# Another order of all engines in the attention step, and two 128x512 products of constants ahead of its stack transposes

## The reference

```python
x = x + tanh(g_xattn) * xattn(layernorm(x), ctx, ctx, mask, ...)   # 16 heads of 8, rope on q and k
x = x + tanh(g_ffn) * ffn(layernorm(x), ...)                       # 8 experts, each token goes to one
# ffn: logits = x @ Wr + br; idx = argmax(logits); gate = softmax(logits)[idx]
#      out = gate * (gelu(x @ W1[idx] + b1[idx]) @ W2[idx] + b2[idx])
```

## Time and profile before

| | us |
|---|---|
| median of 3 runs (lowest, highest) | 294.68 (293.27, 297.7) |
| the profiled execution | 294.33 |
| its span, first to last instruction | 292.5 |
| busy: PE, DVE, ACT, POOL | 237.4, 188.7, 165.9, 178.2 |
| mean granted TensorE clock | 0.942 of full |

### The profile page before, as it was taken

How to read it: one execution, slowest core, us unless ns; L and a number is a source line. 1 busy time by engine, 2 the same in 40 slices (tenths; PEclk the granted TensorE clock), 3 DMA queues, 4 the chain that set the end, 5 groups by cost and what they waited for, 6 DMA issues and landing times.

```text
span 292.5 us, 13366 instructions
## 1 busy us (share of the span) xinstructions
PE 237.4 (81%) x5065; PEld 201.2 (69%) x5065; DVE 188.7 (64%) x638; ACT 165.9 (57%) x482; POOL 178.2 (61%) x221
## 2 busy tenths in 40 slices
PE   1257899888798898879888896788789899999960
PEld 1146777677676676757666675577679899999950
DVE  1636758788789669798888957775576444444420
ACT  1235758788667668567878675335364344444420
POOL 2275745756647859748898686711877755555550
PEclk9999979999799989799999999758999999999995
DMA  7899000303030401204000000132132533111100
GB/s 229 244 380 358 14 2 10 106 13 103 3 112 12 119 16 56 90 2 131 16 12 25 13 26 12 37 89 55 53 116 79 147 108 100 55 30 32 38 20 0
DMA packets 23729, 22.41 MB, mean 77 GB/s; under 512 B 3792, under 2 KB 19173, under 8 KB 23668
## 3 DMA queue, kind: packets, MB, share of 16 engines
q1 hardware_dynamic: 20388, 15.75, 17.6%
q0 software_dynamic: 2272, 4.46, 4.6%
q10 hardware_dynamic: 1008, 1.35, 1.4%
HBM read 16.50 MB, written 5.51 MB: 75 GB/s over the span
## 4 chain that ended last, share of the span: by engine, by line
PE 56%; DVE 19%; issue 11%; POOL 5%; ACT 3%; DMA 2%; SPq 0%; POOLq 0%; DVEq 0%; ACTq 0%
PE ps L734 12%; PE ps L788 10%; DVE mx L1227 8%; PE ps L778 5%; PE ps L745 5%; PE ps L764 5%; PE ps L763 3%; PE ps L717 3%; PE ps L715 3%; PE ps L716 3%; PE ps L810 2%; DMA x_all<-in_x 2%; PE ps L855 2%; PE ps L703 1%; POOL rows L501 1%
## 5 line engine op out<-in xcount | busy, mean ns | idle before, releaser
L549 POOL DMA_INDIRECT out<-fin,got x39 | 37.9, 972 | 27.5 <-DVE fin L1286 22.0
L1227 DVE TENSOR_REDUCE mx<-ps 128x16 f16<-128x1024 f32 x32 | 39.1, 1222 | 18.6 <-PE ps L745 18.1
L501 POOL DMA_INDIRECT rows<-x_all,dest_i x32 | 32.8, 1025 | 19.5 <-DVE x_all L1062 12.3
L734 PE MATMUL ps<-w_f,hT 128*128 x312 | 44.5, 286 | 0.0
L788 PE MATMUL ps<-vx,pr 128*64 128x32 f32 x1024 | 39.5, 234 | 2.8 <-DVE on L1162 2.4
L788 PEld LDWEIGHTS ps<-vx,pr 128*64 128x64 f32 x1024 | 36.0, 150 | 7.1 <-ACT pr L578 2.4
L734 PEld LDWEIGHTS ps<-w_f,hT 128*128 128x128 f32 x312 | 37.8, 191 | 1.0 <-issue 0.3
L528 POOL TENSOR_TENSOR rot<-qk,cf 128x256 f32<-128x256 f32 x32 | 23.4, 730 | 24.7 <-ACT qk L600 17.4
L515 POOL TENSOR_TENSOR stk<-rot,stk 128x256 f16<-128x256 f32 x32 | 21.7, 678 | 25.1 <-DVE stk L1240 25.0
L1286 DVE SCALAR_TENSOR_TENSOR fin<-ps,got 128x128 f32<-128x128 f32 x39 | 13.7, 350 | 36.0 <-PE ps L734 34.9
L578 ACT ACTIVATE pr<-ps 128x1024 f32<-128x1024 f32 x32 | 32.7, 1021 | 6.7 <-PE ps L832 6.7
(11 more groups left out here) (156 smaller groups left out, 615.4 us busy)
## 6 DMA issues: line engine op xcount, KB each, us to landing
got<-rows SPq DMA_DIRECT2D x39, 72.0 KB, 1.9
w_f<-in_W_rows SPq DMA_DIRECT2D x8, 256.0 KB, 3.1
w_r<-in_W_last_row SPq DMA_DIRECT2D x8, 256.0 KB, 4.3
w_f<-in_L_ffn_W SPq DMA_DIRECT2D x8, 256.0 KB, 4.7
x_all<-in_x SPq DMA_DIRECT2D x3, 512.0 KB, 8.3
xt_all<-in_x_t SPq DMA_DIRECT2D x3, 512.0 KB, 7.2
ct_all<-in_ctx SPq DMA_DIRECT2D x3, 512.0 KB, 7.5
out<-fin,got POOLq DMA_INDIRECT x39, 2.3
```

The lines of the kernel that those rows point to most:

```text
L501: pool.indirect_dma_start(out=rows, out_offset=bass.IndirectOffsetOnAxis(ap=dest_i[:, t:t + 1], axis=0), in_=x_all[:, t, :], in_offset=Non ...
L549: pool.indirect_dma_start(out=out_d, out_offset=bass.IndirectOffsetOnAxis(ap=got_i[:, u % GOT, R_ID:R_ID + 1], axis=0), in_=fin[:, u % FRI ...
L734: mm = pe.matmul(o, hT[:, par, c, :], w2_f[:, bass.ds(e, 1), c, :].rearrange("p o n -> p (o n)"), start=False, stop=(c == FC - 1))
L1227: dve.tensor_reduce(mx[:, t % 2, :].rearrange("p (w r) -> p w r", w=4)[:, :, 0:NA], ps_s[:, :].rearrange("p (w a k) -> p w a k", w=4, k=S) ...
```

## The change

Nothing that reaches the output is changed. What moves, in each attention step:

- PE: the transpose of the maxima of tile i-3 (it was tile i-2 at the step's end) and the onT transpose go right behind the projection; the PV product goes ahead of the stacks; the transposed scores go between the two halves of the scores. Ahead of the stacks, from tile 3 on, stand two products of a constant with a constant, 128x512 in fp16, into the bank that the stacks then overwrite (keep_warm).
- ACT: the copy of onT goes ahead of k, k ahead of lx, v ahead of kT and qT.
- DVE: x2 goes ahead of q; the casts hi go ahead of the maximum mx.
- POOL: the scatters go behind the rope.
- The transposed maxima move to bank 7, beside the PV product. For this PE waits for on before it writes the maxima, and for ACT's copy of them before PV. The values get a ring of their own, VRING = 5.

```diff
+VRING = 5
+WARM, WARM_FROM = 2, 3
-        vx = sb("vx", [P, RING, 2, 8, 32])
+        vx = sb("vx", [P, VRING, 2, 8, 32])
-        ps_mx = bank[5].bitcast(F16)[:, 0:P]
+        ps_mx = bank[7].bitcast(F16)[:, 4 * P:5 * P]
...
@@ POOL: step(i) @@
-                for _ in range(SCATTER_AT.get(i, 0)):
-                    scatter()
                 t = i
...
                     pool.tensor_tensor(rot[:, par, :], rot[:, par, :], rot_s[:, par, :], ALU.add).then_inc(rope_done, 1)
+                for _ in range(SCATTER_AT.get(i, 0)):
+                    scatter()
...
@@ ACT: step(i) @@
                     act.activation(mxT[:, t % 2, :], ps_mx, ACT.Copy).then_inc(mxT_ev, 1)
+                t = i - 5
+                if live(t):
+                    act.wait_ge(onT_done, t + 1)
+                    wait(act, op_done, t - 1)
+                    act.activation(onT[:, t % 2, :], ps_onT, ACT.Copy).then_inc(onT_ev, 1)
...
                     act.wait_ge(qe_ev, t + 1)
-                    act.activation(x_all[:, t, R_LOGIT:R_LOGIT + NE], ps_lx, ACT.Copy).then_inc(lx_ev, 1)
...
                     act.activation(qk[:, par, D:2 * D], ps_kv[:, 0:D], ACT.Identity, scale=mask_s[:, t:t + 1]).then_inc(k_ev, 1)
+                    act.activation(x_all[:, t, R_LOGIT:R_LOGIT + NE], ps_lx, ACT.Copy).then_inc(lx_ev, 1)
...
-                    wait(act, pv_done, t - RING + 1)
+                    wait(act, pv_done, t - VRING + 1)
...
@@ PE: step(i) @@
+            def keep_warm(n):
+
+                for _ in range(n):
+                    pe.matmul(bank[5], ident_h, ch[:, K_EXP:K_EXP + 512], start=True, stop=True)
...
+                t = i - 3
+                if live(t):
+                    pe.wait_ge(mx_done, t + 1)
+                    wait(pe, on_done, min(T, i - 4))
+                    wait(pe, mxT_ev, t)
+                    pe.transpose(ps_mx, mx[:, t % 2, :], ident_h).then_inc(mxT_done, 1)
...
+                t = i - 4
+                if live(t):
+                    s, par = t % VRING, t % 2
+                    pe.wait_ge(p_rdy, t + 1)
+                    pe.wait_ge(v_ev, t * 4 + 4)
+                    wait(pe, on_done, t)
+                    pe.wait_ge(mxT_ev, min(T, t + 2))
...
+                t = i - 1
+                if live(t):
+                    par = t % 2
+                    wait(pe, qT_ev, t)
+                    if t >= WARM_FROM:
+                        keep_warm(WARM)
...
-                t = i - 2
-                if live(t):
-                    pe.wait_ge(mx_done, t + 1)
-                    pe.wait_ge(qT_ev, min(T, t + 2))
-                    wait(pe, mxT_ev, t)
-                    pe.transpose(ps_mx, mx[:, t % 2, :], ident_h).then_inc(mxT_done, 1)
...
@@ DVE: step(i) @@
+                t = i - 6
+                if live(t):
+                    dve.wait_ge(op_done, t + 1)
+                    dve.wait_ge(lx_ev, t + 1)
+                    dve.tensor_tensor(x_all[:, t, 0:QX], ps_op, x_all[:, t, 0:QX], ALU.add).then_inc(x2_done, 1)
...
-                t = i - 2
-                if live(t):
-                    dve.wait_ge(s_done, t + 1)
-                    wait(dve, mxT_done, t - 1)
-                    dve.tensor_reduce(mx[:, t % 2, :].rearrange("p (w r) -> p w r", w=4)[:, :, 0:NA],
...
                     dve.tensor_copy(win[:, H:2 * H, :].rearrange("p h (c d) -> p h c d", c=4)[:, :, 1:4:2, :], k_f
                                     ).then_inc(hi_done, 1)
+                t = i - 2
+                if live(t):
+                    dve.wait_ge(s_done, t + 1)
+                    wait(dve, mxT_done, t - 1)
+                    dve.tensor_reduce(mx[:, t % 2, :].rearrange("p (w r) -> p w r", w=4)[:, :, 0:NA],
...
```

More of the change, by code:

```diff
@@ L608, in step @@
                     act.activation(tg[:, :], gates[:, :], ACT.Tanh).then_inc(s_tg, 1)
+                t = i
+                if live(t):
+                    s = t % VRING
+                    wait(act, pv_done, t - VRING + 1)
+                    if t == 0:
+                        act.wait_ge(s_v1, 2)
+                    v_ps = ps_kv[:, D:2 * D].rearrange("p (j hh d) -> p j hh d", hh=2, d=HD)
+                    for b in range(2):
+                        for hh in range(2):
+                            act.activation(vx[64 * hh:64 * hh + 64, s, b, :, 16 * hh:16 * hh + HD],
+                                           v_ps[64 * b:64 * b + 64, :, hh, :], ACT.Copy).then_inc(v_ev, 1)
                 t = i - 1
@@ L616, in step @@
                                    ).then_inc(qT_ev, 1)
-                t = i
-                if live(t):
-                    s = t % RING
-                    wait(act, pv_done, t - RING + 1)
[L621 to L628, removed]
-                if live(t):
-                    act.wait_ge(onT_done, t + 1)
-                    wait(act, op_done, t - 1)
-                    act.activation(onT[:, t % 2, :], ps_onT, ACT.Copy).then_inc(onT_ev, 1)
                 if i - 2 in EXPERT_AT:
@@ L765, in step @@
                     pe.matmul(ps_kv[:, 0:D], pick, bk_h[:, :], start=False, stop=True).then_inc(qkv_done, 1)
+                t = i - 3
[4 more added lines that the diff above has]
+                    pe.transpose(ps_mx, mx[:, t % 2, :], ident_h).then_inc(mxT_done, 1)
+                if i == 3:
+                    pe.wait_ge(s_vo, 64)
+                    pe.matmul(bank[4][:, 0:NE], wo_n[:, :], id_wr[:, P:QX], start=True, stop=True).then_inc(s_wox, 1)
+                t = i - 5
+                if live(t):
+                    if t == 0:
+                        pe.wait_ge(s_cs, 2)
+                    pe.wait_ge(on_done, t + 1)
+                    wait(pe, x2_done, t)
+                    if i - 3 in GROUP_AT:
+                        pe.wait_ge(g_read, GROUP_AT[i - 3] + 1)
+                    pe.transpose(ps_onT, on[:, t % 2, :], ident).then_inc(onT_done, 1)
+                t = i - 4
[5 more added lines that the diff above has]
+                    pe.wait_ge(mxT_ev, min(T, t + 2))
+                    for j in range(8):
+                        for b in range(2):
+                            mm = pe.matmul(ps_o[S * b:S * b + S, 32 * j:32 * j + 32], pr[:, par, NA * (j % 2) + j // 2, b, :],
+                                           vx[:, s, b, j, :],
+                                           start=True, stop=True)
+                    mm.then_inc(pv_done, 1)
                 t = i - 1
@@ L779, in step @@
                     mm.then_inc(stk_done, 1)
[L780 to L791, removed]
                 if tile(i - F0):
@@ L834, in step @@
                     mm.then_inc(st_done, 1)
+                t = i - 2
+                if live(t):
+                    pe.wait_ge(half_done, t + 1)
+                    scores(t, 1).then_inc(s_done, 1)
                 if i - 2 in GROUP_AT:
@@ L1164, in step @@
                                       ALU.mult).then_inc(on_done, 1)
+                t = i - 6
+                if live(t):
+                    dve.wait_ge(op_done, t + 1)
+                    dve.wait_ge(lx_ev, t + 1)
+                    dve.tensor_tensor(x_all[:, t, 0:QX], ps_op, x_all[:, t, 0:QX], ALU.add).then_inc(x2_done, 1)
+                if third is not None:
+                    route_place(third)
                 t = i
@@ L1182, in step @@
                                              in1=w1_h[:, e, :], op0=ALU.mult, op1=ALU.subtract).then_inc(s_w1lo, 1)
[L1183 to L1189, removed]
                 t = i - 6
```

11 lines of the change are left out of this document (4 added, 7 removed).

## The result

| | before | after |
|---|---|---|
| median us of 4 runs each, side by side | 295.19 | 320.15 (317.88 to 321.61) |
| ratio, 95% interval | | 1.0862 (1.0764 to 1.096) |
| span of the profiled execution, us | 292.5 | 318.6 |
| mean granted TensorE clock | 0.942 | 0.922 |

The change makes the kernel slower, as forecast, and by twice the forecast amount: 25 us where the sum had 12.7. The time lies 1 us above the top of the range.

What follows compares the result with a forecast made beforehand. DVE's serial loop through the rope was taken as the bound: 26 x 5.7 + 3.0 + 1.7 = 152.9 against 141.7, +11.2; 294.33 + 11.2 + 1.5 = 307 us, range 297 to 319.

Steps and rivals of the forecast that it cites:

- The loop: DVE's serial chain per attention step, mx through rope and casts to next mx: 5.7 us against 4.95; chance 0.62.
- PE's loop: TensorE's chain per step with the two products at 0.48 us: 5.53 us, 0.17 under 5.7, so covered.
- Hidden edits: POOL's scatter behind the rope (2.5 us to spare), the value ring, v and lx order on ACT: each 0.
- work that stays serial: DVE's tile counts at step 30 and expert biases at step 20, 3.0 us; PE's stalls add 1.7.
- PE's stalls: Stalls inside the transposed scores, 2.2 us in 3, less slack of 0.17 each: 1.7 us added.
- the 13.0 us: Kernel before, steps 5 to 31: excess over 26 x 4.95, mostly DVE's other work, to be hidden by the change.
- behind step 31: After the last rope, PE's loop goes on with the maxima behind on: +1.5 us, bounds -1 to +4.
- The rule on the clock: Products would hold TensorE's clock; worth at most 5 us in the old order, nothing where DVE's loop ends last.
- Within 2%: Rival: clock counts and loops overlap better, or k's wait for onT vanishes; 289 to 298 us, chance 0.20.
- PE is the bound: Rival: PE's work without waits plus products sets the step, 4.4 us, about 272 us; chance 0.08.
- The clock is lost: Rival: PE's single wait per step drops it to half clock in a quarter of steps, +21, 328 us; chance 0.10.
- products at their upper bound: The two constant products at half clock, 0.96 us a step: PE's loop 6.0 us, +8 in 26 steps.

Runs made afterwards that it cites:

- Run 3: Kernel before with one edit, DVE's casts hi placed ahead of the maximum mx: 324.89 us, ratio 1.096, quiet step 6.04 us.
- run 2: Changed kernel with DVE's rden and on taken one step earlier, ahead of the casts: 303.44 us, ratio 1.025, quiet step 5.24 us.
- run 1: Changed kernel without the two 128x512 products, nothing else: 319.97 us, ratio 1.083, quiet step 5.72 us.
- run 6: Changed kernel with the two products in steps 33 to 35 as well: 320.59 us, ratio 1.092.
- Run 5: Changed kernel with DVE's occasional work (memsets, expert biases, tile tables) moved ahead of the casts: 311.04 us, ratio 1.060.
- run 4: Kernel before with one edit, the two products added ahead of the stack transposes from tile 3 on: 294.59 us, ratio 0.991.
- run 7: Changed kernel with DVE's occasional work ahead of the casts and without the two products: 314.0 us, ratio 1.062.

## Why the prediction was right in direction and short in size

**The loop: right, row by row.** Counted from the end of mx at 48.24 in the timeline above: rden at -0.09 (forecast -0.08), on 0.19 (0.20), the maxima's transpose 0.58 (0.55), k 1.34 (1.34), first rope product 1.83 (1.83), sum 3.32 (3.32), casts 4.08 (4.09), next mx 4.49 (4.49), its end 5.71 (5.71). Run 3 shows that the casts ahead of mx make the loop, run 2 that on ahead of the maxima's transpose lengthens it by 0.48.

**PE's loop: right.** The scores end at 52.45, 4.21 behind mx; with a hand-off of 0.02 and mx 5.46, where the forecast had 5.53, so the slack is 0.26. The pair of products takes 0.54 at full clock, not 0.48, and is hidden (run 1). The slack is lost in a stall, as below.

**Hidden edits: right where the rows show it.** POOL's low halves end at 47.84 and their stacks begin at 50.99, 3.1 us to spare. The value ring and the place of lx were read as free and not tried alone.

**A first step that failed: "work that stays serial".** It has 3.0 us for steps 20 and 30, 1.7 for PE's stalls, and nothing for PE at half clock. The memsets of step 8 and the router's logits of step 19 also lie on the loop. From q to q, less 5.72:

| steps | more than a quiet step, us | what the rows show |
|---|---|---|
| 8 | 0.70 | memsets behind mx |
| 19 | 0.97 | logits on DVE, 1.55, which make the casts late |
| 20 | 1.60 | PE at half clock ahead of mx, 0.89; expert biases and a routing row behind mx, 0.71 |
| 30 | 1.90 | tile counts, issue 2.46 |
| 11 to 15 | 2.02 | PE's stalls within the scores |
| 25 to 27 | 1.96 | the same |
| 28 | 1.92 | PE at half clock |

The serial work of DVE comes to 4.3: the blocks that the forecast named took 2.6 of its 3.0, and steps 8 and 19, which it left out, 1.7. PE's stalls were taken as 1.7 and are 4.0. One of them in the chain:

```profile
76.01 0.51 issue
76.52 0.26 PE ps L747 x5
...
76.80 1.24 DVE mx L1248
```

That step is 6.21 us long, 0.49 over the quiet one: the slack of 0.26 did not help, since the five products left took 0.26 us more once PE started again. The half clock had no term at all and took 2.8. In step 20 the stacks take 0.85 instead of 0.45; at step 28 PE has, in the chain, 1.85 for PV (1.13), 0.97 for the products (0.54), 0.85 for the stacks:

```profile
129.51 0.85 PE ps L817 x8
...
177.19 1.85 PE ps L800 x32
179.04 0.97 PE ps L754 x2
180.01 0.85 PE ps L817 x8
```

Together: 26 quiet steps of 5.72 are 148.7 where the sum had 148.2, 0.5 more; serial work 1.3, stalls 2.3, half clock 2.8, and 0.4 spread over the other steps: the 7.3 us. Where the half clock falls is partly chance: run 6, the same code up to step 33, has step 28 at 5.75 us.

Behind this stands one reading. The forecast put most of the 13.0 us by which the kernel before exceeds 26 clean steps down to DVE's other work, and took that as hidden from then on, a gain of 8.3 us. But the clean step of the earlier trace rows already holds such work, among it a difference of expert weights, as the timeline of before shows:

```profile
49.00 0.68 DVE L1181 SCALAR_TENSOR_TENSOR w_l<-w_f,w_h 128x512 f16<-128x512 f32 x1
```

The excess sits in single long steps, made in some of DVE's routing (0.95 and 0.52 us in step 27) and in others of pauses of PE (1.67 us ahead of the stacks in step 12, 1.14 within the transposed scores in step 16), and in the changed kernel 160.2 - 148.7 = 11.5 us of excess are there again. Of the 8.3, 1.5 came.

**The second step that failed: "behind step 31", the largest miss,** 8.6 us where the forecast had 1.5, with bounds of -1 to +4. It reasoned that "there is no rope" there, and so saw no loop; but PE's maxima still wait for on, and on stands behind the tables of steps 31 and 32 (1.95 and 1.32 us of issue, of which 0.58 is usual: 2.1 us). Run 5 takes 6.2 of the 8.6 back and leaves 2.4, near the 1.5. Part of the 6.2 goes with the clock: PV lies on the chain at 198.21 with 1.92 us, at 194.00 in run 5 with 1.12 (both above), and from 220 to 230 us the change runs at half clock, run 5 at full, the window of the change being

```profile
220.00:230.00 10.00, 8.72 (x139) 7.34 (x140) 5.18 (x26) 3.92 (x9) 1.59 (x2) 0.50 0.06 17
```

Whether the clock fell because PE waited for the tables was not tried by itself, so how the 6.2 divides stays open. Run 6 only shows that more PE work in steps 33 to 35 does not bring it back.

**The rule on the clock.** In the rows, the products hold the granted clock: 0.98 against 0.88 from 43 to 180 us in the changed order, 1.00 against 0.96 in the old one. The Trainium skill ("TensorE: Matmul & The Clock Gate", Part 1), by which the array is throttled unless its activity releases it, agrees with this. The products did not hold it everywhere: not from 200 to 230 us in run 6. The forecast that a held clock is worth nothing in the new order holds in its sum (run 1). It does not hold step by step: without the products single steps were longer, 1.1 us in all from step 5 to 31, and behind step 31 the run was 3.0 us shorter, with 0.74 granted from 220 to 230 us instead of 0.50.

**The rivals.** "Within 2%" fell: k's wait for onT is there, and the loops overlap as laid out. "PE is the bound" fell with run 1. "The clock is lost" had a part right, 2.8 us in the loop and more in the tail.

**Two sums in the prediction.** The top of its range, 319, is put down to products at their upper bound, but those add 8 us to 307, which is 315. And DVE's idle time ahead of the casts, 3.4 us, is counted from the start of q; from its end it is 3.1, as measured (49.18 to 52.32). Neither changes the account.

## What to carry to other kernels

When a reorder turns two overlapping loops into one serial loop, list everything that ever stands on that loop, the once-only work and the steps after the last regular one too: here the quiet step was forecast to 0.01 us, and moving once-only work off the loop gave 9 us, a part of it by the clock. Move such work to where its engine waits in every step. Do not count a kernel's long steps as side work that will be hidden before the rows say what made each of them long. Work that only holds the clock gave nothing measurable in either order (runs 1 and 4); look at the quiet step's bound before adding it.

## What the runs showed of the hardware that was not expected

- A product of 128 rows by 512 columns in fp16 takes 0.27 us here (0.54 the pair) at full clock, four times the 0.06 of the earlier trace rows and some, and 0.97 the pair at half clock.
- In the changed order, a mean granted clock between 0.88 and 0.96 moved the time by 0 to 1.6%: 320.46 us at 0.922 and 319.85 us at 0.946 in two executions of the changed kernel, 318.85 us at 0.882 in run 1; 310.0 and 314.97 us in the profiled executions of runs 5 and 7, at 0.961 and 0.902.
- PE's stalls filed under "issue" in the bursts of small score products, 0.2 to 0.8 us, fall in other steps in each kernel (with the change steps 11 and 12 are 6.2 us long, in run 7 they are quiet at 5.72), but in the same ones for the same code (run 6 has 6.20 and 6.27 there). What causes them was not tried.
